# Moving the negated maxima of an attention layer into the transposed q by a 4 KB DMA, in place of a second transposition of q

## The reference

```python
x = x + L0_attn(layernorm(x))            # a state-space block: in-projection, causal convolution, gate, out-projection
x = x + L0_xattn(layernorm(x), ctx)      # cross attention, 16 heads, 64 context rows
x = x + L0_ffn(layernorm(x))             # self attention (16 heads) and a mixture of 8 experts, top 2
x = x + L1_attn(layernorm(x))            # self attention, 16 query heads, 4 key heads
x = x + L1_xattn(layernorm(x), ctx)      # cross attention, 16 query heads, 4 key heads
x = x + L1_ffn(layernorm(x))             # 128 -> 512 -> 128 with gelu
```

## Time and profile before

| | |
|---|---|
| median of 3 runs | 728.47 us (727.01 to 729.55) |
| span of the profiled execution, first to last instruction | 728.7 us |
| PE busy | 634.2 us (87%) |
| DVE busy | 550.5 us (76%) |
| ACT busy | 438.1 us (60%) |
| POOL busy | 178.4 us (24%) |
| mean granted TensorE clock | 0.988 of full speed |

### The profile page before, as it was taken

One profiled execution on the slowest core, in us unless ns is written; L12 is line 12 of the kernel. 1 busy time (PEld: TensorE's weight loads), 2 busy tenths in 40 slices (PEclk: granted clock), 3 DMA queues, 4 the chain that ended last, 5 costly groups with the idle time before them and its releaser, 6 DMA issues.

```text
span 728.7 us, 14858 instructions
## 1 busy us (share of the span) xinstructions
PE 634.2 (87%) x5800; PEld 430.9 (59%) x5800; DVE 550.5 (76%) x1513; ACT 438.1 (60%) x863; POOL 178.4 (24%) x348
## 2 busy tenths in 40 slices
PE   2688899899799998899888997978999899999887
PEld 0255458458556685558645684554567467674556
DVE  7559986858987789776878468899758965777783
ACT  4124666675676646756577544756775678767534
POOL 9614411102132222211241033051132102020202
PEclk9989999999999999999999999999999999999999
DMA  8400000000000000000000000000000000000000
GB/s 298 119 2 9 1 1 1 2 1 1 1 22 2 2 9 7 9 1 1 16 2 1 1 2 15 2 1 1 2 16 2 1 1 1 1 1 2 2 1 22
DMA packets 10358, 10.62 MB, mean 15 GB/s; under 512 B 2832, under 2 KB 9520, under 8 KB 10032
## 3 DMA queue, kind: packets, MB, share of 16 engines
q1 hardware_dynamic: 9568, 6.98, 3.3%
q10 hardware_dynamic: 720, 2.69, 0.9%
HBM read 8.60 MB, written 1.07 MB: 13 GB/s over the span
## 4 chain that ended last, share of the span: by engine, by line
PE 49%; DVE 32%; ACT 11%; issue 4%; POOL 2%; DMA 1%; ACTq 1%; SPq 0%; POOLq 0%; DVEq 0%
DVE qs L1150 8%; PE psA L1562 8%; PE psB L1549 8%; PE psO L1500 6%; ACT P L839 5%; PE psB L1476 4%; PE psA L1460 4%; PE psM L1439 4%; DVE QT L1138 4%; DVE qs L1145 3%; PE psM L1358 3%; PE psM L1315 2%; ACT QT L836 2%; DVE stats L948 1%; DVE kz_s L1131 1%
## 5 line engine op out<-in xcount | busy, mean ns | idle before, releaser
L839 ACT ACTIVATE P<-psB 128x512 f32<-128x512 f32 x320 | 176.9, 597 | 71.5 <-PE psB L1476 46.1
L1150 DVE TENSOR_REDUCE qs<-psA 128x2 bf16<-128x512 f32 x256 | 165.4, 690 | 26.6 <-PE psA L1460 25.4
L1460 PE MATMUL psA<-kz_s,QT 128*128 128x512 bf16 x256 | 90.7, 385 | 13.7 <-DVE qs L1150 8.0
L1476 PE MATMUL psB<-QT,kz_s 128*128 128x256 bf16 x512 | 90.6, 276 | 9.7 <-ACT QT L836 3.2
L846 ACT ACTIVATE P<-psB,W 128x256 f32<-128x256 f32 x160 | 66.4, 473 | 39.8 <-PE psB L1549 34.8
L1439 PE MATMUL psM<-identb,qs 128*128 128x128 bf16 x896 | 72.4, 222 | 11.0 <-DVE qs L1145 2.9
L1439 PEld LDWEIGHTS psM<-identb,qs 128*128 128x128 bf16 x896 | 56.3, 99 | 31.6 <-issue 8.0
L1500 PE MATMUL psO<-P,vp 128*32 128x256 f32 x1024 | 68.3, 385 | 2.1 <-ACT P L839 1.5
L1476 PEld LDWEIGHTS psB<-QT,kz_s 128*128 128x128 bf16 x512 | 39.2, 98 | 52.2 <-ACT P L839 26.3
L1562 PE MATMUL psA<-w,P 128*128 128x128 f32 x512 | 66.1, 277 | 1.8 <-ACT P L846 0.9
L661 POOL TENSOR_SCALAR veps<-mv 128x2 f32<-128x2 f32 x40 | 10.4, 261 | 229.2 <-DVE mv L952 228.6
(11 more groups left out here) (178 smaller groups left out, 1109.8 us busy)
## 6 DMA issues: line engine op xcount, KB each, us to landing
w<-expert_w ACTq DMA_DIRECT2D x2, 1024.0 KB, 10.3
toep<-decay_rows SPq DMA_DIRECT2D x4, 512.0 KB, 5.9
x<-x SPq DMA_DIRECT2D x8, 128.0 KB, 2.8
y<-base SPq DMA_DIRECT2D x8, 128.0 KB, 1.9
W<-weights SPq DMA_DIRECT2D x1, 940.0 KB, 6.9
rows<-bias_rows SPq DMA_DIRECT2D x1, 872.0 KB, 10.4
ctxp<-context SPq DMA_DIRECT2D x8, 64.0 KB, 2.1
fw<-mlp_w ACTq DMA_DIRECT2D x2, 256.0 KB, 10.9
```

Source lines behind the costliest of these rows:

```text
L839: act.activation(P[:, p, :, :].rearrange("p a s -> p (a s)"), psB[:, s.u % B_BANKS, :], ACT.Exp, scale=LAYERS[s.L]["scale"]).then_inc(b_dr ...
L1150: dve.tensor_reduce(qs[L["W"]][j][:, t * H + h:t * H + h + 2, 0], ps.rearrange("p (h c) -> p h c", h=2), AX.X, ALU.max, negate=True).then_ ...
L1460: ins = pe.matmul(ps, QT[j][:, h // L["HB"], t * 128:t * 128 + 128], kz[s.L][j][:, kv:kv + 2, :].rearrange("p h s -> p (h s)"), start=True ...
L1476: ins = pe.matmul(ps[:, i * S:i * S + S], kz[s.L][j][:, kv + i, kc * 128:kc * 128 + 128], QT[j][:, h // L["HB"], :], start=True, stop=True)
```

## The change

Q stays as it was. A now writes the negated maxima into a small tile of their own, `negmax` (128 rows x 2 halves x 16 values, bf16), in the order in which the rows of `QT` need them. M becomes three parts: PE transposes one 128x16 tile (one instruction in place of 8 or 4); DVE (cross) or ACT (self) copies 16x128 values out of `psM` into `negmaxT`; SP waits for that copy and issues a DMA of 16 rows of 256 bytes, 4 KB in all, from `negmaxT` into the two (x0, x1, s1) or four (s0) partitions of `QT` that belong to the slots. S waits for the DMA's semaphore `max_moved` in place of the copy. The memset of the slots in P3 is left for s0 alone (8 of 32 stay). SP gets an order of its own of 75 steps (64 M, 8 H, 3 C), and the orders of PE, DVE, ACT and POOL are new. The number of sets stays at three.

```diff
-    if s.kind in ("Q", "M"):
-        return ("PE", "ACT") if query_on_scalar(s) else ("PE", "DVE")
+    if s.kind == "Q":
+        return ("PE", "ACT") if s.q == 1 and not is_cross(s) else ("PE", "DVE")
+    if s.kind == "M":
+        return ("PE", "DVE", "SP") if is_cross(s) else ("PE", "ACT", "SP")
...
 ORDER = {
     "PE": (
...
-        "ghh7h7h7hghh655hh5hhf6hhh6h5h5f6fhff76f7f7f7756666g56gg65g7g77gg7hghh776hh6hh65h57576765767767"
+        "h7h7hh77ghh555gfhh6hh5f6hhh6hh6f5hff767ff777f566656g667gg577gg7hgg7h7hghh656hh6h57576766577767"
...
+    "SP": (
+        "aabbwaabbacacaabbx0ccbbd1dccddcceed2dyeedd3efefggeeffg4hhghhffgghhffgghh657"
+    ),
...
+    if engine == "SP" and s.kind == "M":
+        out[f"max_moved{s.j}_{s.q}"] = 16
...
+        negmaxT = [v[0:16, 0:128].bitcast(BF16).rearrange("p (h c) -> p h c", h=2) for v in y1]
+        negmax = both("negmax", [128, 2, 16], BF16)
...
+        def maxima(s):
+
+            L, half, n = LAYERS[s.L], s.q // (2 if is_cross(s) else 8), H // LAYERS[s.L]["HB"] // 2
+            tile = negmax[s.j][:, half, :]
+            if L["cross"]:
+                lo = s.q % 2 * 4
+                return tile.rearrange("p (a m) -> p a m", a=L["HB"])[:, :, lo:lo + 4]
+            h, t = scores_of(s)
+            lo = h // L["HB"] % n * T + t
+            return tile.rearrange("p (a m) -> p a m", a=L["HB"])[:, h % L["HB"]:h % L["HB"] + 2, lo]
...
-            for s in order["DVE"]:
-                if s.kind == "C" and s.L == "x1" and s.q == 0 and s.b + 2 < B:
+            for s in order["SP"]:
+                if s.kind == "M":
+                    m, f, b, c = s.misc
+                    sp.wait_ge(misc_drained[m], c)
+                    groups = groups_of(s)
+                    sp.dma_start(QT[s.j][0:128:LAYERS[s.L]["W"], groups[0]:groups[0] + len(groups), :],
+                                 negmaxT[s.j][:, s.q, :]).then_inc(max_moved[s.j][s.q], 16)
+                if s.kind == "C":
...
+                if s.kind == "M":
+                    m = free(s)
+                    act.copy(negmaxT[j][:, s.q, :], bf(m)[0:16, 0:128]).then_inc(misc_drained[m], 1)
...
-                    mark(dve.memset(tile[:, :, 0:MS], 0.0))
+                    if s.L == "s0":
+                        mark(dve.memset(tile[:, :, 0:MS], 0.0))
...
+                if s.kind == "M":
+                    m = filled(s)
+                    dve.tensor_copy(negmaxT[j][:, s.q, :], bf(m)[0:16, 0:128]).then_inc(misc_drained[m], 1)
...
+                        dve.tensor_reduce(maxima(s), ps.rearrange("p (m a c) -> p a m c", a=2, c=C), AX.X, ALU.max,
                                           negate=True).then_inc(a_drained, 1)
...
+                if s.kind == "M":
+                    a = previous(s, "A", s.L, 2 * s.q + 1 if L["cross"] else 8 * s.q + 7).a
+                    if ahead(a_drained, a + 1):
+                        pe.wait_ge(a_drained, a + 1)
+                    m = take(s)
+                    pe.transpose(bf(m)[0:16, 0:128], negmax[j][:, s.q, :], identb[:, :]).then_inc(misc_filled[m], 1)
...
-                                lo = (2 * t + i) * 128
+                                lo = (2 * i + t) * 128
...
-                    drained(previous(s, "M", s.L, s.q // 2 if L["cross"] else s.q // 8))
+                    half = s.q // (2 if L["cross"] else 8)
+                    moved = previous(s, "M", s.L, half).after[f"max_moved{j}_{half}"]
+                    if ahead(max_moved[j][half], moved):
+                        pe.wait_ge(max_moved[j][half], moved)
```

More of the change, by code:

```diff
@@ L132, in engines @@
         return ("DVE", "ACT") if is_cross(s) else ("DVE", "ACT", "POOL")
-    if s.kind in ("Q", "M"):
-        return ("PE", "ACT") if query_on_scalar(s) else ("PE", "DVE")
+    if s.kind == "Q":
+        return ("PE", "ACT") if s.q == 1 and not is_cross(s) else ("PE", "DVE")
+    if s.kind == "M":
+        return ("PE", "DVE", "SP") if is_cross(s) else ("PE", "ACT", "SP")
     if s.kind == "C":
-        return ("PE", "DVE") if s.q else ("PE", "DVE", "POOL")
+        return ("PE", "DVE") if s.q else ("PE", "DVE", "POOL", "SP") if s.L == "x1" and s.b + 2 < B else ("PE", "DVE", "POOL")
     if s.kind == "F3":
@@ L139, in engines @@
     if s.kind == "H":
-        return ("PE", "DVE") if s.L == "s0" else ("PE", "DVE", "POOL")
+        return ("PE", "DVE") if s.L == "s0" else ("PE", "DVE", "POOL", "SP")
     if s.kind == "R1":
@@ L422, in decoder @@
         ot_drained = [sem(f"ot_drained{o}") for o in range(2)]
+        max_moved = [[sem(f"max_moved{j}_{half}") for half in range(2)] for j in range(SLOTS)]
         weights_loaded = sem("weights_loaded")
@@ L567, in _ @@
                     load_context(s.b // 2 + 1)
-                if s.kind == "H" and s.L == "f":
+                if s.kind == "H":
                     store(s)
@@ L1424, in _ @@
                     ins.then_inc(misc_filled[m], 1)
[L1425 to L1428, removed]
-                            pe.wait_ge(q_split, split)
-                    else:
-                        a = previous(s, "A", s.L, 2 * s.q + 1 if L["cross"] else 8 * s.q + 7).a
-                        if ahead(a_drained, a + 1):
-                            pe.wait_ge(a_drained, a + 1)
+                if s.kind == "M":
[4 more added lines that the diff above has]
+                    pe.transpose(bf(m)[0:16, 0:128], negmax[j][:, s.q, :], identb[:, :]).then_inc(misc_filled[m], 1)
+                if s.kind == "Q":
+                    split = previous(s, "P3", s.L).after["q_split"]
+                    if ahead(q_split, split):
+                        pe.wait_ge(q_split, split)
                     m = take(s)
```

60 lines of the change are left out of this document (27 added, 33 removed).

## The result

The change makes the kernel slower: 742.67 us (median of 4 runs, 741.74 to 743.02) against 729.01 for the kernel before on the same chip (727.01 to 734.7), a ratio of 1.0167 with a 95% interval of 1.0133 to 1.0201. Forecast were 713 us and a range of 695 to 737, so the time lies outside the range, on the other side of no change. It happens to be the time that the rival of the late DMA gave (743), but that is chance: the DMA is not late.

The account below looks back on a forecast made before the run. PE, busy 87% of the span, was nearest to a bound, with a path hopping between PE, DVE and ACT. 728.7 - 23 (transposes) - 5 (copies) + 12 (waits for the DMA) = 712.7, so 713 us; range 695 to 737.

Parts of the forecast that it names:

- the rival of the late DMA: S on PE waits for a landing that the steps between do not cover; 743 us at 2.8 us; chance 0.17.
- the cover: PE's other work between M and S, 5 steps in the median where it was 3, hides the DMA.
- the transposes: M on PE loses 384 transposes; taken as 23 us gained, 31 by the group's busy time.
- rival of the hidden gain: DVE's reductions set the pace at A; transposes worth 13 us, copies nothing; 728 us, no change; chance 0.13.
- The copies: M's shorter copies on DVE and ACT; 5 us gained, between nothing and 8.
- The DMA and the waits: M to S: the DMA takes 1.9 us, the way 2.45; S waits 20 us, 12 more than before.
- covered waits: Rival: the DMA lands in about 1.3 us, S waits 9 us, as now; 701 us; chance 0.14.
- the reckoning by steps of 0.56 us: An M with n steps behind it leaves S waiting max(0, way - 0.56 n); 8.2 us before, 20 after.
- SP's 64 issues: DMA issues on SP's queue at 0.38 to 0.47 us, 24 to 30 us in all; cost put at nothing.

Follow-up runs that it names:

- e3: The changed kernel, in its new orders, without the DMA (maxima left out of the turned q, the exponentials' scale a twentieth): 740.39 us.
- e4: The changed kernel without the DMA (maxima left out, scale a twentieth), in the orders of the kernel before: 722.51 us.
- w4: e3 (new orders, no DMA) with 59 added matmuls put into PE's waits to hold the clock: 741.18 us.
- w3: e4 (old orders, no DMA) with 48 added matmuls at 26 of PE's steps to hold the clock: 722.78 us.
- s1: e4 with PE's order alone changed: the first two S behind each M put up to three steps later (107 swaps): 748.68 us.
- c1: e4 with M on PE as in the kernel before, so 384 transposes more, the small copy kept: 725.11 us.
- e8: e4 with each maximum taken over half of its columns, exponentials whole: 708.37 us.
- e1: The changed kernel with its DMA, in the orders of the kernel before, SP's moves in the order of PE's M steps: 777.67 us.
- v3: e3 with PE's order alone changed: V put up to three steps behind its last S (23 swaps): 756.40 us.
- e2: The kernel before, with its second turn of q, in the new orders of PE, DVE, ACT and POOL: 775.50 us.

## Why the prediction was wrong

*The new orders, and the cover that they buy, were costed at nothing.* This is the step that failed, and the transposes below are the second: "What covers it is PE's other work, and the order was rewritten: 5 steps in the median stand between M and S, where it was 3." The sum counted the steps as work that PE has to do anyway. They are, but they were taken from other places: counted in the orders, the mean from the last S to its V fell from 3.0 steps to 2.5, and from the last A of a half to its M from 5.5 to 4.3. Measured, the new orders cost 18 us without any DMA (e3 against e4), with the clock held too (w4 against w3); a crude lengthening of the same distance costs 26 (s1). This alone is more than the 16 us of gain that the sum gave. Shown is the price of the new orders as a whole; that it is the price of the cover is argued, from s1.

*PE's transposes were not worth 23 us.* This term failed by as much: c1 says 0 to 3. PE was busy for 87% of the span, but that didn't price them, and neither did the chain. The M of the earlier trace rows stands on the chain of the kernel before, where by PE's order of steps 17 us are M's transposes; in c1 M's line has 3% of the chain, some 20 us; and without them the time hardly changes. PE's busy time fell by 12 us in the old orders (e4, 622.3) and by 7 in the new (e3, 626.8), not by 23 to 31. In part the other matmuls took longer at a lower granted clock: the 256 of self layers' A were busy for 90.7 us before, 93.8 in e4 (clock 0.976) and 91.0 in w3 (0.998). The prediction's rival of the hidden gain had the mechanism, DVE's reductions setting the pace where A stands, and still gave the transposes 13. Its argument against that rival, that all engines were made lighter by 3 to 4%, did not hold: a reduction that sets the pace was not made lighter. Halving the reductions gave 14 us in the old orders (e8), shorter M 8.

*The copies, put at 5 us,* were not measured alone. c1 gains 6 us on the kernel before, and in this stand S's waits for the copies too, which fell from 6.9 us to 1.7. If those waits count in full, about 1 us is left for the copies and M's shorter hold of its bank, and the 5 was too much.

*The DMA and the waits.* The 1.63 us from the issue to S (1.63 to 1.67 in the five waits) were within the bounds, near the middle of 1.3 (covered waits) and 1.9 (taken). S waits 3.5 us and not 20: with a way of 2.14 the reckoning by steps of 0.56 us gives 4 x 1.58 + 3 x 1.02 + 8 x 0.46 = 13, so the steps that stand there now must be longer than the mean one, or PE meets the wait elsewhere before. So this term was -3 and not +12, and beside it, unseen, stood +18. That a wait of S counts in full was right (e1: 52 us of waits, 55 of cost). SP's 64 issues cost next to nothing: the change lies over e3 by 2 us, S's waits for the DMA included.

The sum with measured terms: 729 - 7 for M, with its waits, + 18 for the orders + 2 for the DMA and SP = 742; 742.67 was measured. Added up so, it takes both wrong terms to make the change slower: with the orders free it would be 724, with some 21 us more from the transposes 721, both still under the kernel before. The waits, reckoned 15 us too long, hid a part of the error by luck.

*What was said to show it wrong* did: "if PE's idle time grows elsewhere, by the new orders on DVE and ACT or by a clock that falls where PE waits". Idle time grew from 94.5 us to 113 (e3, whose record is complete: 739.9 - 626.8); the clock fell too, but with it held the orders differ as much.

What stays open: which places in the new orders, and which engine's strings, make the 18 us beyond the meetings with the exponentials and reductions. Half or more of it lies before the first store; no run changes the order in that stretch alone, or PE's new strings without those of the other engines. v3 and s1 show that steps put late in a sequence can cost far more than the waits which they save.

## What to carry to other kernels

In a pipeline whose order is written out, latency is hidden by distance, and distance is taken from other pairs of steps: price the cover by running the new order without the latency that it is for. An engine's share of busy time doesn't price its work, nor does its share of the chain: take one engine's part away and leave the rest, as c1 does, before counting on it. A wait's name tells where the loss shows; moving V away from its wait for P took 3 us off that wait and cost 16.

## What the runs showed of the hardware

A 4 KB move within SBUF from SP's queue took 1.63 us from the start of its issue to the waiting matmul (1.63 to 1.67 in the five waits), less than the 1.9 to 2.8 us from issue to landing of moves of 16 to 128 KB; its issue took 0.50 us on SP where those of a store and a load took 0.38 and 0.47. The granted clock can be held at 0.99 and more by work in waits (0.976 to 0.998 between e4 and w3), and that gave no time here. The same 5,800 matmuls were busy for 634.2 us in the old orders (granted clock 0.988) and 647.3 in the new (e2, 0.974):

```profile
PE 647.3 (84%) x5800; PEld 435.7 (56%) x5800; DVE 552.2 (71%) x1513; ACT 434.5 (56%) x861; POOL 177.7 (23%) x348
```
